# Order of TensorE's work around the low-rank feed-forward and the entries to attention and MLP

## What is computed

```python
# block 0, behind its attention
h = layernorm(x) * (1 + cb) + sb
P = h @ U1                       # 256 -> rank 64
H = gelu(P @ V1 + b1)            # 64 -> 1024
x = x + gb * ((H @ U2) @ V2 + b2)  # 1024 -> 64 -> 256
# block 1: performer attention (relu features, causal prefix sums), then a dense MLP
h = layernorm(x) * (1 + ca) + sa
n = layer_norm(h, ln1)           # queries, keys and values come from n
a = attention(n) + h
y = layer_norm(a, ln2)
x = x + ga * (a + ... gelu(y @ w1 + b1) @ w2 ...)
# then a feed-forward over chosen tokens
```

## Time and profile before

| | |
|---|---|
| median of three runs | 1878.65 us |
| the profiled execution | 1879.73 us, its span 1878.5 us |
| TensorE busy | 1765.5 us, 94% of the span |
| VectorE busy | 1261.6 us, 67% |
| ScalarE busy | 895.0 us, 48% |
| GpSimd busy | 698.3 us, 37% |
| mean granted clock of TensorE | 0.992 |
| chain that ended last | TensorE 62%, DMA issue and DMA 18%, VectorE 13% |

### The profile page before, as it was taken

The page is one execution under the profiler, slowest core; times in us unless marked ns, Lnnn a source line. Parts: engine busy times, 40 slices in busy tenths (PEclk is TensorE's granted clock), DMA queues, the critical chain, the costliest instruction groups (busy, mean ns, idle before and its releaser), DMA issues.

```text
span 1878.5 us, 41287 instructions
## 1 busy us (share of the span) xinstructions
PE 1765.5 (94%) x16417; PEld 1253.3 (67%) x16417; DVE 1261.6 (67%) x2771; ACT 895.0 (48%) x1967; POOL 698.3 (37%) x1090
## 2 busy tenths in 40 slices
PE   7999998998999999999899999999988999999998
PEld 4766775667666667566856666756675666765667
DVE  4688857644688885762677887486367888757545
ACT  4476724223466672523356666242245676533223
POOL 2455534050055564213115555323212555521410
PEclk9899999999999999999999999999999999999999
DMA  8566650050266665013146666303115666520500
GB/s 229 120 154 157 143 146 36 2 90 26 80 147 145 146 140 153 1 31 61 36 105 147 143 143 142 122 1 65 27 35 130 146 145 146 137 97 1 91 1 24
DMA packets 128561, 182.65 MB, mean 97 GB/s; under 512 B 33297, under 2 KB 89329, under 8 KB 127345
## 3 DMA queue, kind: packets, MB, share of 16 engines
q1 hardware_dynamic: 114928, 173.72, 38.3%
q10 hardware_dynamic: 13440, 6.30, 1.2%
HBM read 62.44 MB, written 4.24 MB: 35 GB/s over the span
## 4 chain that ended last, share of the span: by engine, by line
PE 62%; SPq 14%; DVE 13%; ACT 5%; DMA 4%; issue 2%; POOL 1%; DVEq 0%; POOLq 0%
SPq L943 14%; PE scores L449 12%; PE bank L449 7%; PE bank L657 6%; PE scores L637 5%; PE bank L694 4%; DVE prob L771 4%; DMA placed<-prob 3%; PE scores L1664 2%; PE scores L1577 2%; PE scores L1048 2%; ACT prob L871 2%; PE scores L1105 2%; PE scores L420 1%; PE scores L1224 1%
## 5 line engine op out<-in xcount | busy, mean ns | idle before, releaser
L871 ACT ACTIVATE prob<-prob,neg_max 128x768 f32<-128x768 f32 (+5 forms) x384 | 273.6, 713 | 95.7 <-DVE neg_max L763 95.7
L657 PEld LDWEIGHTS bank<-placed,v_t 128*64 128x64 f32 x4608 | 253.6, 138 | 93.2 <-issue 93.2
L657 PE MATMUL bank<-placed,v_t 128*64 128x128 f32 x4608 | 275.9, 276 | 33.1 <-DMA placed<-prob 24.0
L637 PE MATMUL scores<-k_t,q_t 64*128 64x128 f32 (+10 forms) x2176 | 288.0, 410 | 0.0
L287 POOL TENSOR_TENSOR rstd<-rstd,minus_half 128x2 f32<-128x2 f32 x96 | 69.4, 725 | 556.0 <-DVE rstd L286 555.6
L771 DVE STREAM_TRANSPOSE prob<-prob 128x1536 f32<-128x1536 f32 x128 | 225.2, 1772 | 29.8 <-ACT prob L871 29.3
L833 POOL COPY placed<-prob 32x768 f32<-32x768 f32 x256 | 210.7, 823 | 19.6
L637 PEld LDWEIGHTS scores<-k_t,q_t 64*128 64x128 f32 x2176 | 165.1, 187 | 72.0 <-issue 61.2
L763 DVE CUSTOM_DVE_ANT_1 prob<-scores,hx 128x128 f32<-128x128 f32 (+4 forms) x320 | 165.3, 576 | 54.0 <-PE scores L637 30.1
L820 POOL COPY rec_wide<-rec 128x128 f32<-128x128 f32 x256 | 65.4, 291 | 330.1 <-DVE rec L775 233.2
L871 ACT ACTIVATE hx<-hx,neg_max 128x896 f32<-128x896 f32 (+1 forms) x128 | 119.5, 934 | 77.6 <-DVE neg_max L763 76.8
(11 more groups left out here) (247 smaller groups left out, 3330.9 us busy)
## 6 DMA issues: line engine op xcount, KB each, us to landing
placed<-prob SPq DMA_DIRECT2D x768, 96.0 KB, 2.2
placed<-hx SPq DMA_DIRECT2D x384, 96.0 KB, 2.1
f<-in_L_ffn_f SPq DMA_DIRECT2D x16, 2048.0 KB, 13.4
x<-in_L_attn_x SPq DMA_DIRECT2D x8, 512.0 KB, 4.4
mod_rows<-mod_scratch SPq DMA_DIRECT2D x32, 128.0 KB, 5.5
out<-x SPq DMA_DIRECT2D x16, 256.0 KB, 2.1
w_ring<-in_L_attn_w_q ACTq DMA_DIRECT2D x24, 128.0 KB, 3.0
w_ring<-in_L_attn_w_kv_up ACTq DMA_DIRECT2D x48, 64.0 KB, 2.2
```

Of the source, the lines that this page charges most:

```text
L637: last = nc.tensor.matmul(score_tiles[head][:, at_ // 512, at_ % 512:at_ % 512 + count], q_t[buf][rows_, tile * P:(tile + 1) * P], k_of[bu ...
L657: last = nc.tensor.matmul(out_bank[rows_, at_:at_ + P], v_t[pair % 2][:, j, rows_], placed[m % 2][:, :, head, first_block(m, i) + j, :], s ...
L871: nc.scalar.activation(p_, p_, ACT.Exp, scale=-1.0, bias=neg_max[:, k:k + 1], accum_out=row_sum[:, k:k + 1]).then_inc(flow["exp_done"], 1)
```

## The change

Only the order of calls changes, and the order of matmuls within `feed_wide`:

- `feed_wide` takes two banks at a time and issues high, high, low, low for two blocks where it issued high, low, high, low.
- The turn of the low half comes before the last of the four output products of attention (tile 6). That product's first 14 matmuls stand between the turn and the rank product, its last 2 behind the rank product. So `norm_stats` of the high half, which needs tile 6, is called behind `feed_rank` of the low half.
- `feed_rank` of the high half comes before `feed_output` of the low half.
- `attention_turn` of the low half comes before `feed_output` of the high half; its two copies on ScalarE so come before the write of the ones in `v_tok` (L1453).
- `attention_turn` of the high half comes before `tile_numerators(0)` and `tile_state(0)`.
- `mlp_turn` of the high half comes before the last of the four tiles of `mlp_output` of the low half (`to_residual` calls `between` there).

```diff
--- before.py
+++ after.py
@@ -990,7 +990,7 @@
 
             wrote = []
             for t in tiles_of(half):
-                if between and t == half * TH + 1:
+                if between and t == (half + 1) * TH - 1:
                     between()
                 i, ps, reader = banks.take()
                 done = multiply(ps[:, 0:D], pieces(slice(t * P, (t + 1) * P)), reader, *deps, turned=wide)
@@ -1091,8 +1091,20 @@
 
         def feed_wide(half, split):
 
-            return blocks(FM, lambda m, cols: [(v1_split[:, m * P:(m + 1) * P], r[:, cols]) for r in (rank_high, rank_low)],
-                          half, P, gelu_into(hid, b1_0), turned=split)
+            cols, evacuate, wide = slice(half * HW, (half + 1) * HW), gelu_into(hid, b1_0), []
+            for m in range(0, FM, 2):
+                taken = [banks.take() for k in range(2)]
+                done = {}
+                for part_, r in enumerate((rank_high, rank_low)):
+                    for k, (i, ps, reader) in enumerate(taken):
+                        w = v1_split[:, (m + k) * P:(m + k + 1) * P]
+                        done[k] = pe.do(lambda e, w=w, ps=ps, r=r, part_=part_: nc.tensor.matmul(
+                            ps, w, r[:, cols], start=part_ == 0, stop=part_ == 1), split[part_], reader)
+                for k, (i, ps, reader) in enumerate(taken):
+                    step = evacuate(m + k, cols, ps, done[k])
+                    banks.read_by(i, step)
+                    wide.append(step)
+            return wide
 
         QUARTER = HW // 2
 
@@ -1433,22 +1445,26 @@
         bias_x(0, low_norm)
         late = sorted(tiles_of(1), key=lambda t: OUT_ROUND[t])
         wrote = [next(output5)]
-        for t in late[1:]:
+        for t in late[1:-1]:
             *_, step = head_output(t)
             wrote.append(step)
+        feed_turned = feed_turn(0, low_norm)
+        last_output = head_output(late[-1])
+        next(last_output)
+        rank0 = feed_rank(0, feed_turned)
+        wrote.append(next(last_output))
         inv = norm_stats(x, 1, wrote, EPS, tiles=late)
-        rank0 = feed_rank(0, feed_turn(0, low_norm))
         wide0 = feed_wide(0, rank0)
         high_norm = norm_apply(x, inv)
         bias_x(1, high_norm)
         feed_turned = feed_turn(1, high_norm)
         rank2_0 = feed_rank2(0, wide0)
+        rank1 = feed_rank(1, feed_turned)
         norms = attention_norms(0, feed_output(0, rank2_0))
-        next(norms)
-        rank1 = feed_rank(1, feed_turned)
         *_, attn_norm = norms
         wide1 = feed_wide(1, rank1)
         rank2_1 = feed_rank2(1, wide1)
+        attn_turned = attention_turn(0, attn_norm)
         norms = attention_norms(1, feed_output(1, rank2_1))
         ones_set.append(act.do(lambda e: nc.scalar.mul(
             v_tok[:, :, :, HD1:VPAD], minus_half[:, 0:1].unsqueeze(2).unsqueeze(3).to_broadcast([P, T, HEADS1, VPAD - HD1]), -2.0)))
@@ -1456,7 +1472,6 @@
         banks7 = Banks(all_banks[0:7])
         banks7.readers, banks7.at = banks.readers[0:7], (banks.at if banks.at < 7 else 6)
         banks = banks7
-        attn_turned = attention_turn(0, attn_norm)
         for step in range(3):
             next(norms)
         split = {0: attention_queries(0, attn_turned)}
@@ -1482,11 +1497,12 @@
                 k7 = attention_keys(7, attn_turned)
             if t == TH:
                 attention_keys_turned(6, k6, k7)
+            if t == 0:
+                attn_turned = attention_turn(1, attn_norm)
             copying = tile_numerators(t, masked, state)
             if t + 1 < T:
                 state = tile_state(t, state)
             if t == 0:
-                attn_turned = attention_turn(1, attn_norm)
                 split[1] = attention_queries(1, attn_turned)
             if t == 1:
                 k5 = attention_keys(5, attn_turned)
@@ -1510,9 +1526,10 @@
         banks = Banks(all_banks)
         banks.readers = readers
         LOW, MIDDLE, HIGH = tuple(range(TH)), (TH, TH + 1), (TH + 2, TH + 3)
-        slots_normed = [normalise(x, 0, mlp_output(0, wide0), EPS)]
+        mlp_turned = []
+        slots_normed = [normalise(x, 0, mlp_output(0, wide0, lambda: mlp_turned.append(mlp_turn(1, mlp_norms[1]))), EPS)]
         slots_h = slot_rows_of(LOW, slots_normed[0])
-        wide1 = mlp_wide(1, mlp_turn(1, mlp_norms[1]))
+        wide1 = mlp_wide(1, mlp_turned[0])
         low_turned = slot_turn(LOW, slots_normed[0])
```

## The result

The changed kernel took 1892.08 us (median of seven runs, 1886.98 to 1897.38), the kernel before 1878.55 us in seven runs beside it: a ratio of 1.0079, 95% interval 1.0059 to 1.0099. It is slower, by 13.5 us between the medians; the forecast was 1889 in a range of 1880 to 1894, from a base of 1878.65.

A forecast was written before the change was run, and what follows sets the result against it. TensorE, busy 94% of the span, was taken as the bound. Terms 1.55 + 0.35 + 0.45 - 0.50 + 0.80 gave 2.65 us per batch, 10.6 over four batches: 1889 us, range 1880 to 1894.

The forecast's parts named there:

- Steps 1 and 2: First turn ahead of last attention output, feed_wide in pairs: turn waits 0.40 us, first feed_wide ends 0.97 us earlier.
- Step 3: Second feed-forward turn: statistics now behind rank_low, so TensorE waits 1.2 us and ends the turn at 295.2 instead of 294.81.
- Step 4: Second rank product ahead of first output product: VectorE's adds start later, last norm before attention ends 1.3 us later.
- step 5: Attention's first turn ahead of second output product: TensorE some 4 us idle per batch, queries 1.55 us later.
- step 6: From queries to first scores: VectorE's later adds delay the turned keys' copy, +0.35 us per batch (0 to 0.6).
- Step 7: Attention's high-half turn ahead of first numerators: waits for norms queued behind VectorE's masks, +0.45 us per batch (0.2 to 0.7).
- Step 8: MLP turn before the last output tile: its wait and the restart go, -0.50 us per batch (-0.6 to 0).
- Step 9: TensorE's clock falls behind the wait at attention's first turn in every batch: +0.8 us per batch (0 to 1.7).
- (a): Rival: VectorE waits come but the clock holds; 1.85 us per batch, 1886 us; chance 0.25.
- (b): Rival: later stages take up most of the loss; -0.5 to +0.6 us per batch, 1877 to 1881; chance 0.12.
- (c): Rival: products hide their waits, VectorE's order costs nothing; 6.7 us less per batch, 1852; chance 0.12 with half-way case.
- (d): Rival: cold clock also slows VectorE's chain; over 1.7 us per batch, 1894 us and above; chance 0.06.

The follow-up runs named there:

- e4: Changed kernel with the statistics of the high half's tiles 5 and 7 called before the rank product; 1884.48 us, ratio 1.0048 to the kernel before.
- e1: Changed kernel with three products that nobody reads added on TensorE in front of attention's first turn; 1885.63 us, ratio 1.0055 to the kernel before.
- e9: Changed kernel without VectorE's second operation of the low half's modulated rows (output differs); 1880.00 us, ratio 1.0038 to the kernel before.
- e3: Changed kernel with the second rank product back behind the first output product; 1878.21 us, ratio 1.0025 to the kernel before.
- e10: Kernel before with only the second rank product and attention's first turn moved ahead of the first and second output products; 1890.41 us, ratio 1.0082.
- e8: Changed kernel, moving only what has inputs ready: e3, e4, e2, attention's second turn before the state update, MLP's first turn earlier; 1863.31 us, 0.9935 to the kernel before.
- e2: Changed kernel with attention's first turn back behind the feed-forward's second output product; 1888.44 us, ratio 1.0073 to the kernel before.

## Why the prediction was right

**Steps 1 and 2 held.** Counted from the first turn, the high piece was to be used after 7.05 us and the low one after 7.76; it was 7.01 and 7.74. The turn waited 0.34 for its fourth tile (0.40 was said).

**Step 3 held.** TensorE waited 1.13 us at the second turn (1.2), rank2 began 13.54 behind the first turn (13.47). e4 takes the wait away by moving two statistics.

**Step 4 held, 0.3 us long.** The output product came after 19.05 us (18.70): rank2 and the rank product took 3.60 and 1.91 where I had 3.51 and 1.72. The last norm ended 32.20 behind the first turn (32.07).

**Steps 5 and 6 held in mechanism and, without the clock, in size.** The wait before the turn is there, 3.22 us in one piece and 0.20 behind it. The two steps together were 1.90 per batch; e1, which has the order without the cold clock, shows 2.15: 1.89 for step 5, where I had 1.55, and 0.26 for step 6, where I had 0.35 (its own rows add up to 0.31), with the wait for the turned keys that it names. e9 shows that the chain on VectorE sets the wait, e3 that its start does, e10 that these two moves are enough.

**Step 7 held:** 0.55 for 0.45, of which 0.10 came back between Q1 and A, which I had not counted. **Step 8 held in mechanism:** -0.69 for -0.50, past its bound of -0.6. From this turn to the next product it is 0.87 us (873.42 to 874.29), where it was 1.47, wait included; and the first group behind the wait had been 0.1 us longer than it is now without one.

**Step 9 was mis-sized.** The clock fell in every batch, as said, but it cost 1.81 us per batch where I took 0.8; the upper bound of 1.7 was passed. Against e1, the way to the queries was 1.36 us longer and the queries themselves 0.66 (4.44 instead of 3.70 in the first batch), 2.02 together, where I had 1.1. One part of the miss is the single cold stretch: it cost 1.6 us in each of the two batches that had one (second and third). The other is that in the first and fourth batch the clock stayed down for 6.8 us and not for 3.4, which cost 2.3 and 2.6. That step 6's wait would hide a part of it was right: the wait for the turned keys that e1 has in front of its first scores is gone in three of the four batches of the changed kernel, and takes 0.2 off.

The sum was 2.65 per batch, the stretches give 3.71, so over four batches I was 4.2 us short. The total came nearer: the span grew by 11.9 us where I had 10.6, and the median came out 3 us above the forecast. That is luck in part, since the stretches outside the touched stages, which I had taken as unchanged, happened to be 3 us shorter in the profiled execution.

The rule of the Trainium skill ("TensorE: Matmul & The Clock Gate", "HAM oscillation — how this bites in real kernels"), that a wait between groups of matmuls lets the next group start cold, held in the changed kernel: the granted clock was 0.50 behind the wait of 3.2 us in all four batches, and e1 shows its price.

**The rivals.** (a), no fall of the clock, is out, since it fell in every batch; what it would have been is e1, 53.42 from F to the first scores against 55.23. (b), the later stages take up the loss, is out: the attention loop gave only 0.10 back. (c), every covered wait is worth its length, fell with the normalised tiles, which came as late as step 3 and step 4 say, and with e3, where two uncovered waits made the kernel faster. (d), over 1.7 by the clock, happened by a little, and the total still came out in the range. Its own time was worked out wrongly: with 1.7 the terms add up to 3.55 per batch, 1893, and not 1894.

What stays open: which part of the 3 us outside the touched stages belongs to the change. The cold stretches at the end of a batch came in two of four batches before, in three of four after, in two with e1 and e8, in all four with e3; no run here separates that from chance.

## What to carry to other kernels

Before putting a product ahead of another to cover a wait, find who is fed by the one that is pushed back: here waits of TensorE of 0.7 and 0.5 us were cheaper than starting a 12 us chain on VectorE 1 us later, since the next turn stood at the end of that chain (e3). A turn is worth moving ahead only up to the place where its last tile is ready; there a short product behind it was enough cover (in e8 the state update, 0.6 us). And in an order written out by hand, a step stands behind everything that was called before it, ready or not: two statistics called earlier took the wait at the second turn away (e4).

## What the runs showed of the hardware

- A wait of TensorE can cost more than its length: behind the 3.2 us of wait in the changed kernel the granted clock was 0.50 in all four batches, and that cost another 1.8 us per batch (e1).
- TensorE need not be idle all the time before such a fall, and the wait can be shorter: with a wait of 1.6 us the clock fell in all four batches of e2 (busy for 1.37 to 1.57 of the 3.41 us before it), with 1.41 us in two of the four batches of e9 (busy for 1.66 of 3.41). With 0.68 us, in e3, the entry stayed at full clock in all four.
- The clock can stay down for 6.8 us in one piece, as in two of the four batches of the changed kernel. TensorE was busy there for 2.50 and 3.21 of the first 3.41 us, and for all of them in the two batches in which the clock came back.
- The seven runs of the changed kernel spread over 10.4 us and those of before over 6.8, but 23 later runs of the kernel before spread over 11.0; that the falls make the times scatter more is not shown.
- Filling a wait with products that nobody reads made a kernel faster, by 7.2 us in the stretches and 0.24% by the ratios, whose intervals overlap.
